# Moving the rounding of the samples between VectorE's two passes in a deformable-convolution block on one Trainium2 core

## The chip, the cores and the metric

The kernel runs on one NeuronCore of one Trainium2 chip. The metric is the device time of one execution in microseconds. Before the change it is 2600.68 us, the median of three runs (2598.38 to 2600.81).

## The reference

For x of shape (4, 128, 80, 80) in float32:

```python
out_normal = _conv(x, w_normal)
offset = jnp.concatenate([_conv(x, w_offx), _conv(x, w_offy)], axis=1)
out_x = _deform_conv(x, offset, w_dx)
out_y = _deform_conv(x, offset, w_dy)
out = _conv(jnp.concatenate([out_normal, out_x, out_y], axis=1), w_fusion)
out = jax.nn.relu(_bn(out, ...))
out = _bn(_conv(out, w_conv2), ...)
return jax.nn.relu(out + x)
```

`_conv` is a 3x3 convolution with padding 1. `_deform_conv` reads, for each pixel and each of nine taps, four neighbouring pixels at a position that the offsets shift, blends them bilinearly and multiplies the blend with that tap's 128x128 weights. Both deformable convolutions use the same offsets, so they share their samples.

## The kernel before

The work goes in strips of 8 rows (640 pixels), 10 strips to an image, 40 in all, and four more steps empty a pipeline: in step i the offsets of strip i+1, the samples and deformable products of strip i, the fusion convolution of strip i-2 and the last convolution of strip i-4 are worked on. Every engine runs a list of its own, written out by hand, and the engines meet at semaphores alone. `run_steps` runs the steps, and inside one, each engine's `step` runs nine **tap steps**, k = 0 to 8. Tap n = 9i + k is counted through all strips.

Values are kept as a rounded high part (fp32r) and a low part (value minus high), and every product is three matmuls (`three`, L388, L391, L394). What happens to tap m of the samples, in five tiles of 128 pixels:

1. GpSimd gathers five tiles of cells from HBM (`gather`, L350, into 15 slots; a slot is free when the mix has read it).
2. The vertical mix, here **mix**: in strips 0 to 9 ScalarE multiplies the upper half (`upper`) and VectorE adds the lower (L756); from strip 10 on the table holds slopes and VectorE does it alone, with five instructions of L756 on 128x256.
3. The horizontal blend: ScalarE multiplies the left half into `samp` (`left`, five products on 128x128), and VectorE adds the right half (L762, five instructions), here **blend**.
4. TensorE turns the five tiles into PSUM (`turn_samples`, L431, tile `turned`), here **turn**.
5. ScalarE rounds `turned` to `samp_hi` (`samples_high`), and VectorE subtracts (`samples_low`, L708) to `samp_lo`, here **low**.
6. TensorE multiplies (`deform_tap`, tile `acc`).

In tap step k, with n = 9i + k, TensorE turns tap n+1, does a slice of the other convolutions (`SLICES`) and multiplies tap n. Its turn waits for two things, the blends of tap n+1 and the low part of tap n, since there is one `turned`:

```python
at_least(eng, samp_done, TILES * n + TILES)
at_least(eng, samp_lo_done, n)
```

In the same tap step ScalarE makes the left products of tap n+2 and the high part of tap n+1, and then what else the step holds (the upper products of tap n+3 in the first image, evacuations of PSUM, the high parts of sums and differences). VectorE mixes and blends tap n+2, takes the low part of tap n+1, and then does the rest of its step: in tap step 3 (2 in the first four steps) `indices` for the next strip, 14 small instructions from L725 to L742, which wait for ScalarE's copy of the offsets (`turned_evac`, tile `off_s`); in tap steps 4 to 7 the sums, differences and their low parts (L832, L708) and the bank evacuations (L929 to L955); in 0 and 1 the residual (L970). The slopes (L832 on `slope`) are made in tap steps 2 and 6 of the first 27 steps. TensorE's second batch of fusion products in tap step 3 reuses the PSUM bank from which `off_s` is copied, so it waits for that copy too.

Of the kernel before, what the change touches and what calls it, by code (L numbers as in the profile page):

```python
# [15 lines left out]
TAPS = 9  # L16
# [122 lines left out]
def at_least(eng, sem, value):  # L139

    if isinstance(value, int) and value <= 0:
        return
    eng.wait_ge(sem, value)


def deform_block(nc, x, xflat, xpair, weights, bn, const, out):
    ctx = ExitStack()
    with ctx:
# [100 lines left out]
        def strip_const(c, n):  # L249
            return cst[:, per_strip + 4 * c + n:per_strip + 4 * c + n + 1]  # L250
# [280 lines left out]
        def _(eng):  # L531
# [45 lines left out]
            def samples_high(n, tp):  # L577
                at_least(eng, samp_turned, n + 1)
                at_least(eng, tap_done, n - 1)
                copy(samp_hi[:, tp], turned[:, 0:PIX]).then_inc(samp_hi_done, 1)  # L580
# [41 lines left out]
            def step(i, par, fl):  # L622
                for k in range(TAPS):
                    n = i * TAPS + k
                    tp = (par + k) % 2
                    if fl.strip and k < TAPS - 2:
                        left(n + 2, k + 2, par, tp)
                    elif fl.strip and fl.nxt:
                        left(n + 2, k + 2 - TAPS, 1 - par, tp)
                    if fl.strip and (k < TAPS - 1 or fl.nxt):  # L630
                        samples_high(n + 1, 1 - tp)
                    if k in fl.weights:
                        weights_high(fl.weights[k])

                    if fl.strip and k < TAPS - 3:
                        upper(n + 3, i, k + 3, par, 1 - tp)
                    elif fl.strip and fl.nxt:
                        upper(n + 3, i + 1, k + 3 - TAPS, 1 - par, 1 - tp)
                    if k == fl.turn and fl.nxt:
                        turned_evac(i + 1)  # L640
                    if k == 1 and fl.last_row:
                        at_least(eng, last_done, i - 1)
                        copy(d_hi[:, :, Z_ROWS - 1, 1:1 + W], d_raw[:, :, Z_ROWS - 1, 1:1 + W])\
                            .then_inc(last_hi, 1)
                    for job, q in fl.done[k]:
                        if job == "O" and fl.nxt:
                            off_evac(i + 1, q)
                        if job == "F" and q == 0 and fl.fuse:
                            s = i - 2
                            at_least(eng, f_done, T * s + 1)  # L650
                            at_least(eng, mid_lo_done, s)
                            eng.activation(mid_odd, work[0][:, 0:HALF].rearrange("p (r w) -> p r w", w=W), ACT.Identity,
                                           bias=scale1[:, 1:2], scale=scale1[:, 0:1]).then_inc(f_one, 1)
                        if job == "F" and q == 1 and fl.rows:
                            sums_high(i - 1)
                        if job == "F" and q == T - 1:
                            s = i - 2
                            if fl.mtop:
                                at_least(eng, mid_lo_done, s)
                                at_least(eng, c_done, 2 * (s - 2) + 2)  # L660
                                copy(mid[:, par, :, 0, 1:1 + W], mid[:, 1 - par, :, ROWS, 1:1 + W].bitcast(F32),
                                     scale=strip_const(s, 2)).then_inc(mtop_done, 1)
                            if fl.fuse:
                                at_least(eng, f_three, s + 1)
                                at_least(eng, f_four, s + 1)
                                at_least(eng, c_done, 2 * (s - 2) + 2)
                                eng.activation(mid[:, par, 0, 1:1 + ROWS, 1:1 + W], mid_f[:], ACT.Relu)\
                                    .then_inc(mid_hi_done, 1)
                            if fl.rows:
                                zs_high(i - 1)  # L670
                            if fl.mbot:
                                at_least(eng, mid_lo_done, s + 1 if fl.fuse else s)
                                at_least(eng, c_done, 2 * (s - 3) + 2)
                                copy(mid[:, 1 - par, :, SLOT_ROWS - 1, 1:1 + W], mid[:, par, :, 1, 1:1 + W].bitcast(F32),
                                     scale=strip_const(s - 1, 3)).then_inc(mbot_done, 1)
                        if job == "N" and fl.strip:
                            rows = slice(q * HR, q * HR + HR)
                            at_least(eng, sums_done, 6 * i)
                            at_least(eng, zs_done, 7 * i)
                            at_least(eng, keep_done, i)  # L680
                            at_least(eng, n_done, 2 * i + q + 1)
                            copy(raw[:, 0, rows, :], work[q][:, 0:HALF].rearrange("p (r w) -> p r w", w=W))\
                                .then_inc(n_out, 1)
                            if q == 1 and fl.load:
                                x_high(i + 2, par)
                        if job == "C" and fl.second:
                            s = i - 4
                            at_least(eng, c_out, 2 * s + q + 1)
                            part = resid[:, q * HALF:(q + 1) * HALF]
                            eng.activation(part, part, ACT.Relu, bias=scale1[:, 3:4]).then_inc(out_ready, 1)  # L690
                if fl.strip:
                    at_least(eng, tap_done, TAPS * i + TAPS)
                    for d in range(2):
                        for half in range(2):
                            rows = slice(half * HR, half * HR + HR)
                            copy(raw[:, 1 + d, rows, :],
                                 acc[2 * d + half][:, 0:HALF].rearrange("p (r w) -> p r w", w=W)).then_inc(acc_out, 1)

            run_steps(eng, step)


# [3 lines left out]
        def _(eng):  # L705
# [36 lines left out]
                eng.tensor_scalar(index[:, par], above[:, 0], strip_const(s, 1), None, ALU.add).then_inc(idx_ready, 1)  # L742
                eng.wait_ge(idx_ready, s + 1)

            def sample(n, k, par, tp):

                for j in range(TILES):
                    g, turns = (k * TILES + j) % GSLOTS, (k * TILES + j) // GSLOTS + 1
                    both = mixed[:, tp, j].rearrange("p (x c) -> p x c", x=2)
                    base = both  # L750
                    if n < STRIPS * TAPS:
                        at_least(eng, upper_done, TILES * n + j + 1)
                    else:
                        at_least(eng, cells_in[g], (PER // GSLOTS * 16) * (n // TAPS) + 16 * turns)
                        base = corner[:, g, :, 0, :]
                    eng.scalar_tensor_tensor(  # L756
                        out=both, in0=corner[:, g, :, 1, :], scalar=wgt[:, par, 1, 0, j, k:k + 1], in1=base,
                        op0=ALU.mult, op1=ALU.add,
                    ).then_inc(mixed_done, 1)
                for j in range(TILES):  # L760
                    at_least(eng, left_done, TILES * n + j + 1)
                    eng.scalar_tensor_tensor(  # L762
                        out=samp[:, tp, j], in0=mixed[:, tp, j, C:2 * C],
                        scalar=wgt[:, par, 1, 1, j, k:k + 1], in1=samp[:, tp, j], op0=ALU.mult, op1=ALU.add,
                    ).then_inc(samp_done, 1)

            def samples_low(n, tp):
                at_least(eng, samp_hi_done, n + 1)
                low(samp_lo[:, tp], turned[:, 0:PIX], samp_hi[:, tp]).then_inc(samp_lo_done, 1)
# [29 lines left out]
            eng.wait_ge(cst_in, 16)  # L799
            indices(0, 0)  # L800
            weights_low(W_DEF)
            sample(0, 0, 0, 0)
            x_low(1, 1)
            sample(1, 1, 0, 1)
            samples_low(0, 0)

            eng.wait_ge(bn_in, 16)
# [92 lines left out]
            def step(i, par, fl):  # L900
                for k in range(TAPS):
                    n = i * TAPS + k
                    tp = (par + k) % 2
# [1 line left out]
                        last_row(i - 2)  # L905

                    if fl.strip and k < TAPS - 2:
                        sample(n + 2, k + 2, par, tp)
                    elif fl.strip and fl.nxt:
                        sample(n + 2, k + 2 - TAPS, 1 - par, tp)  # L910
                    if fl.strip and (k < TAPS - 1 or fl.nxt):
                        samples_low(n + 1, 1 - tp)
                    if k in fl.transform:
                        weights_form()
# [117 lines left out]
```

## Time and profile before

| what | value |
|---|---|
| median of three runs | 2600.68 us |
| the profiled execution, its time | 2602.97 us |
| its span | 2601.2 us |
| mean granted TensorE clock (share of full) | 0.961 |
| busy: TensorE matmul / weight load | 91% / 89% |
| busy: VectorE / ScalarE / GpSimd | 87% / 60% / 74% |
| mean DMA rate | 217 GB/s |

Busy shares are averages over the span. Rows of the timeline give the start, the busy time and, in brackets, the idle time of the engine before the instruction with what ended it. Consecutive instructions of one engine overlap in their records, so the step from one start to the next is shorter than the busy time.

### The profile page before, as it was taken

The numbers are of one execution on the slowest core, as the hardware profiler recorded it, in microseconds if no ns is written. First come the engines' busy times: TensorE is split into PE (matmuls) and PEld (weight loads), VectorE is DVE, ScalarE is ACT, GpSimd is POOL, SyncE is SP. The second block draws the span as 40 slices with busy tenths as digits, with TensorE's granted clock in tenths as the row PEclk, the third lists the DMA queues.
The fourth block names the chain that finished last, engine by engine and source line by source line (L and its number), as shares of the span: only waits on it lengthen the run. The fifth ranks groups of instructions, "written<-read, shape, count | busy, mean of one in ns | idle before, by whom it ended". The sixth has DMA issues, their size and how long they took to land.

```text
span 2601.2 us, 47091 instructions
## 1 busy us (share of the span) xinstructions
PE 2355.7 (91%) x15680; PEld 2319.4 (89%) x15680; DVE 2265.0 (87%) x5999; ACT 1561.9 (60%) x3577; POOL 1917.4 (74%) x1807
## 2 busy tenths in 40 slices
PE   3668999999999999999999999999999998999997
PEld 3668889898999999998999999999999998999997
DVE  5788988888999999999999989999999998999962
ACT  5777888778555555555555555555555555555531
POOL 7777777777777777777777777777777777777730
PEclk7789999999999999999999999999999999999998
DMA  7767777777777777777777777777777667776630
GB/s 232 220 208 219 235 228 231 232 231 229 227 237 233 231 234 237 233 236 232 236 237 237 234 237 239 238 222 210 209 209 217 206 208 212 210 210 210 202 111 26
DMA packets 179139, 564.90 MB, mean 217 GB/s; under 512 B 32720, under 2 KB 34128, under 8 KB 178768
## 3 DMA queue, kind: packets, MB, share of 16 engines
q0 software_dynamic: 144000, 471.97, 60.3%
q1 hardware_dynamic: 34896, 89.91, 10.1%
q8 instruction: 125, 2.05, 0.3%
q14 instruction: 118, 0.97, 0.1%
HBM read 527.41 MB, written 34.34 MB: 216 GB/s over the span
## 4 chain that ended last, share of the span: by engine, by line
DVE 46%; PE 23%; ACT 15%; issue 8%; DMA 5%; POOL 2%; ACTq 0%; DVEq 0%; SPq 0%; POOLq 0%
DVE mixed L756 11%; DVE d_lo L708 7%; DVE d_lo_f L832 7%; DVE samp L762 6%; ACT samp L535 6%; PE work L388 5%; PE work L394 5%; PE work L391 5%; DMA cells<-slope_table,index 4%; DVE samp_lo L708 4%; ACT samp_hi L534 3%; ACT mixed L535 3%; PE turned L431 2%; POOL cells L350 2%; PE acc L388 2%
## 5 line engine op out<-in xcount | busy, mean ns | idle before, releaser
L350 POOL DMA_INDIRECT cells<-slope_table,index x1350 | 1434.0, 1062 | 414.1 <-issue 223.3
L535 ACT ACTIVATE samp<-mixed,wgt 128x128 f32<-128x128 f32 x1800 | 644.6, 397 | 492.6 <-DVE mixed L756 490.8
L350 POOL DMA_INDIRECT cells<-in_xpair,index x450 | 473.7, 1053 | 166.6 <-issue 83.4
L756 DVE SCALAR_TENSOR_TENSOR mixed<-cells,wgt 128x256 f32<-128x256 f32 x1350 | 560.9, 477 | 39.2 <-DMA cells<-slope_table,index 37.9
L762 DVE SCALAR_TENSOR_TENSOR samp<-mixed,wgt,samp 128x128 f32<-128x128 f32 x1800 | 513.8, 345 | 39.1 <-ACT samp L535 38.8
L388 PE MATMUL work<-d_hi,w_hi 128*128 128x320 f32 x1440 | 467.9, 325 | 22.0 <-ACT off_s L534 19.7
L391 PE MATMUL work<-d_lo,w_hi 128*128 128x320 f32 x1440 | 452.8, 314 | 0.0
L394 PE MATMUL work<-d_hi,w_lo 128*128 128x320 f32 x1440 | 452.3, 314 | 0.0
L388 PE MATMUL acc<-samp_hi,w_hi 128*128 128x320 f32 x1440 | 450.2, 313 | 0.0
L391 PE MATMUL acc<-samp_lo,w_hi 128*128 128x320 f32 x1440 | 448.4, 311 | 0.0
L394 PE MATMUL acc<-samp_hi,w_lo 128*128 128x320 f32 x1440 | 446.9, 310 | 0.0
L431 PE MATMUL turned<-cst,samp 128*128 128x128 f32 x1800 | 267.2, 281 | 194.6 <-DVE samp_lo L708 176.8
L431 PEld LDWEIGHTS turned<-cst,samp 128*128 128x128 f32 x1800 | 214.9, 143 | 223.1 <-issue 151.8
L708 DVE TENSOR_TENSOR samp_lo<-turned,samp_hi 128x640 fp32r<-128x640 f32 x360 | 294.3, 818 | 47.6 <-ACT samp_hi L534 47.6
L388 PEld LDWEIGHTS work<-d_hi,w_hi 128*128 128x128 f32 x1440 | 272.4, 189 | 27.8 <-ACT off_s L534 25.2
L534 ACT ACTIVATE d_hi<-d_lo_f 128x1920 fp32r<-128x1920 f32 (+2 forms) x120 | 153.2, 1277 | 237.7 <-DVE d_lo_f L832 230.9
L388 PEld LDWEIGHTS acc<-samp_hi,w_hi 128*128 128x128 f32 x1440 | 275.9, 192 | 0.0
L391 PEld LDWEIGHTS acc<-samp_lo,w_hi 128*128 128x128 f32 x1440 | 274.9, 191 | 0.0
L394 PEld LDWEIGHTS acc<-samp_hi,w_lo 128*128 128x128 f32 x1440 | 274.8, 191 | 0.0
L391 PEld LDWEIGHTS work<-d_lo,w_hi 128*128 128x128 f32 x1440 | 273.3, 190 | 0.0
L394 PEld LDWEIGHTS work<-d_hi,w_lo 128*128 128x128 f32 x1440 | 272.7, 189 | 0.0
L534 ACT ACTIVATE samp_hi<-turned 128x640 fp32r<-128x640 f32 x360 | 247.8, 688 | 13.4 <-PE turned L431 11.9
(86 smaller groups left out, 4279.3 us busy)
## 6 DMA issues: line engine op xcount, KB each, us to landing
cells<-slope_table,index POOLq DMA_INDIRECT x1350, 3.9
slope<-in_xpair SPq DMA_DIRECT2D x54, 384.0 KB, 5.3
slope_table<-slope SPq DMA_DIRECT2D x54, 384.0 KB, 4.1
x_raw<-in_xflat SPq DMA_DIRECT2D x40, 410.0 KB, 4.1
resid<-in_x SPq DMA_DIRECT2D x40, 320.0 KB, 5.3
out<-resid SPq DMA_DIRECT2D x40, 320.0 KB, 3.9
cells<-in_xpair,index POOLq DMA_INDIRECT x450, 3.8
w_lo_f<-in_weights SPq DMA_DIRECT2D x4, 576.0 KB, 7.9
```

The lines of the kernel that those rows point to most:

```text
L350: eng.indirect_dma_start(out=cells[:, g, :], out_offset=None, in_=cell_rows, in_offset=bass.IndirectOffsetOnAxis(ap=index[:, par, j, k:k + ...
L388: ins = eng.matmul(dst, w_hi[:, w], hi, start=start, stop=False, skip_group_check=True)
L391: ins = eng.matmul(dst, w_hi[:, w], lo, start=False, stop=False, skip_group_check=True)
L394: return eng.matmul(dst, w_lo[:, w], hi, start=False, stop=stop, skip_group_check=True)
L431: ins = eng.transpose(turned[:, j * 128:(j + 1) * 128], samp[:, tp, j, :], ident)
L534: return eng.activation(dst, src, ACT.Copy)
L535: return eng.activation(dst, src, ACT.Copy, scale=scale)
L708: return eng.tensor_tensor(dst, src, hi.bitcast(F32), ALU.subtract)
L756: eng.scalar_tensor_tensor(out=both, in0=corner[:, g, :, 1, :], scalar=wgt[:, par, 1, 0, j, k:k + 1], in1=base, op0=ALU.mult, op1=ALU.add, ...
L762: eng.scalar_tensor_tensor(out=samp[:, tp, j], in0=mixed[:, tp, j, C:2 * C], scalar=wgt[:, par, 1, 1, j, k:k + 1], in1=samp[:, tp, j], op0 ...
L832: return eng.scalar_tensor_tensor(out=dst, in0=a, scalar=1.0, in1=b, op0=ALU.mult, op1=op)
```

## The change

No instruction is added or taken away, and TensorE's, GpSimd's and SyncE's lists stay as they are. `sample` is cut into `mix` (the loop with L756) and `blend` (the loop with L762 before, L765 after). VectorE takes the low part of tap n+1 between mix and blend of tap n+2, and ScalarE rounds tap n+1 before it makes the left products of tap n+2. The three taps ahead of the first step keep their order.

```diff
                     tp = (par + k) % 2
+                    if fl.strip and (k < TAPS - 1 or fl.nxt):
+                        samples_high(n + 1, 1 - tp)
                     if fl.strip and k < TAPS - 2:
                         left(n + 2, k + 2, par, tp)
                     elif fl.strip and fl.nxt:
                         left(n + 2, k + 2 - TAPS, 1 - par, tp)
-                    if fl.strip and (k < TAPS - 1 or fl.nxt):
-                        samples_high(n + 1, 1 - tp)
...
                     if fl.strip and k < TAPS - 2:
-                        sample(n + 2, k + 2, par, tp)
+                        mix(n + 2, k + 2, par, tp)
+                        samples_low(n + 1, 1 - tp)
+                        blend(n + 2, k + 2, par, tp)
                     elif fl.strip and fl.nxt:
-                        sample(n + 2, k + 2 - TAPS, 1 - par, tp)
-                    if fl.strip and (k < TAPS - 1 or fl.nxt):
+                        mix(n + 2, k + 2 - TAPS, 1 - par, tp)
+                        samples_low(n + 1, 1 - tp)
+                        blend(n + 2, k + 2 - TAPS, 1 - par, tp)
+                    elif fl.strip and k < TAPS - 1:
                         samples_low(n + 1, 1 - tp)
```

VectorE in tap steps 2 and 3 of a strip from the eleventh on, before (`resid` closes tap step 1, L725 opens the indices; mixed is the mix, samp the blend):

```order
L970 SCALAR_TENSOR_TENSOR resid<-work1,scale1,resid 128x320
L756 SCALAR_TENSOR_TENSOR mixed<-cells,wgt 128x256 x5
L762 SCALAR_TENSOR_TENSOR samp<-mixed,wgt,samp 128x128 x5
L708 TENSOR_TENSOR samp_lo<-turned,samp_hi 128x640
L708 TENSOR_TENSOR d_lo<-d_lo_f,d_hi 128x3x80
L832 SCALAR_TENSOR_TENSOR slope<-slope 128x3x128
L756 SCALAR_TENSOR_TENSOR mixed<-cells,wgt 128x256 x5
L762 SCALAR_TENSOR_TENSOR samp<-mixed,wgt,samp 128x128 x5
L708 TENSOR_TENSOR samp_lo<-turned,samp_hi 128x640
L725 TENSOR_TENSOR off_s<-off_s 128x5x18
```

and the same place after the change:

```order
L979 SCALAR_TENSOR_TENSOR resid<-work1,scale1,resid 128x320
L756 SCALAR_TENSOR_TENSOR mixed<-cells,wgt 128x256 x5
L708 TENSOR_TENSOR samp_lo<-turned,samp_hi 128x640
L765 SCALAR_TENSOR_TENSOR samp<-mixed,wgt,samp 128x128 x5
L708 TENSOR_TENSOR d_lo<-d_lo_f,d_hi 128x3x80
L837 SCALAR_TENSOR_TENSOR slope<-slope 128x3x128
L756 SCALAR_TENSOR_TENSOR mixed<-cells,wgt 128x256 x5
L708 TENSOR_TENSOR samp_lo<-turned,samp_hi 128x640
L765 SCALAR_TENSOR_TENSOR samp<-mixed,wgt,samp 128x128 x5
L725 TENSOR_TENSOR off_s<-off_s 128x5x18
```

The five blends have moved behind the low part, in every tap step; what follows the group of three is where it was.

ScalarE at the same place, before (L535 is the left products, `samp_hi` the high part, `off_s` the copy of the offsets):

```order
L534 ACTIVATE off_c<-work0 32x320 x3
L535 ACTIVATE samp<-mixed,wgt 128x128 x5
L534 ACTIVATE samp_hi<-turned 128x640
L534 ACTIVATE off_c<-work1 32x320 x3
L535 ACTIVATE samp<-mixed,wgt 128x128 x5
L534 ACTIVATE samp_hi<-turned 128x640
L534 ACTIVATE off_s<-work1 128x270
L652 ACTIVATE mid_f<-work0,scale1 128x4x80
```

and after:

```order
L534 ACTIVATE off_c<-work0 32x320 x3
L534 ACTIVATE samp_hi<-turned 128x640
L535 ACTIVATE samp<-mixed,wgt 128x128 x5
L534 ACTIVATE off_c<-work1 32x320 x3
L534 ACTIVATE samp_hi<-turned 128x640
L535 ACTIVATE samp<-mixed,wgt 128x128 x5
L534 ACTIVATE off_s<-work1 128x270
L652 ACTIVATE mid_f<-work0,scale1 128x4x80
```

The five left products now stand behind the rounding, and so between it and the copy of the offsets.

## Rows read from the trace of the kernel before

**Rows 1.** The page, part 1: busy time, share of the span, instructions of each engine.

```profile
PE 2355.7 (91%) x15680; PEld 2319.4 (89%) x15680; DVE 2265.0 (87%) x5999; ACT 1561.9 (60%) x3577; POOL 1917.4 (74%) x1807
```

**Rows 2.** The page, part 4: the chain that ended last, shares by engine.

```profile
DVE 46%; PE 23%; ACT 15%; issue 8%; DMA 5%; POOL 2%; ACTq 0%; DVEq 0%; SPq 0%; POOLq 0%
```

**Rows 3.** Waits over the whole span: waiter, releaser, us in total, times, longest.

```profile
PE turned L431 <- DVE samp_lo L708: 176.8, 105, 11.9
...
DVE samp_lo L708 <- ACT samp_hi L534: 47.6, 139, 2.1
DVE samp L762 <- ACT samp L535: 38.8, 79, 2.4
```

**Rows 4.** Timeline of TensorE: first turn and one wait of tap steps, strips apart.

```profile
702.97 0.71 PE L431 MATMUL turned<-cst,samp 128*128 128x128 f32 x5
...
1500.66 0.71 PE L431 MATMUL turned<-cst,samp 128*128 128x128 f32 x5
...
1503.95 0.41 PE L388 MATMUL work<-d_hi,w_hi 128*128 128x320 f32 x1 [0.78 <-ACT off_s L534]
...
1563.14 0.71 PE L431 MATMUL turned<-cst,samp 128*128 128x128 f32 x5
...
1569.96 0.71 PE L431 MATMUL turned<-cst,samp 128*128 128x128 f32 x5
...
1597.24 0.74 PE L431 MATMUL turned<-cst,samp 128*128 128x128 f32 x5 [2.54 <-DVE samp_lo L708]
...
1624.16 0.71 PE L431 MATMUL turned<-cst,samp 128*128 128x128 f32 x5
...
2422.44 0.71 PE L431 MATMUL turned<-cst,samp 128*128 128x128 f32 x5
```

**Rows 5.** Timeline of VectorE, two strips of the third image.

```profile
1501.92 0.52 DVE L756 SCALAR_TENSOR_TENSOR mixed<-cells,wgt 128x256 f32<-128x256 f32 x1 [2.32 <-DMA cells<-slope_table,index]
...
1504.41 0.24 DVE L725 TENSOR_TENSOR off_s<-off_s 128x90 f32<-128x90 f32 x1
...
1562.41 1.39 DVE L762 SCALAR_TENSOR_TENSOR samp<-mixed,wgt,samp 128x128 f32<-128x128 f32 x5
1564.62 0.82 DVE L708 TENSOR_TENSOR samp_lo<-turned,samp_hi 128x640 fp32r<-128x640 f32 x1 [0.82 <-ACT samp_hi L534]
1565.37 0.24 DVE L725 TENSOR_TENSOR off_s<-off_s 128x90 f32<-128x90 f32 x1
...
1570.72 1.40 DVE L762 SCALAR_TENSOR_TENSOR samp<-mixed,wgt,samp 128x128 f32<-128x128 f32 x5
1572.04 0.81 DVE L708 TENSOR_TENSOR samp_lo<-turned,samp_hi 128x640 fp32r<-128x640 f32 x1
...
1578.59 1.52 DVE L762 SCALAR_TENSOR_TENSOR samp<-mixed,wgt,samp 128x128 f32<-128x128 f32 x5 [0.19 <-ACT samp L535]
1580.35 0.82 DVE L708 TENSOR_TENSOR samp_lo<-turned,samp_hi 128x640 fp32r<-128x640 f32 x1 [0.23 <-ACT samp_hi L534]
...
1588.24 0.55 DVE L832 SCALAR_TENSOR_TENSOR slope<-slope 128x384 f32<-128x384 f32 x1
...
1596.27 0.82 DVE L708 TENSOR_TENSOR samp_lo<-turned,samp_hi 128x640 fp32r<-128x640 f32 x1 [0.23 <-ACT samp_hi L534]
```

**Rows 6.** Timeline of ScalarE, tap step 3 of the same second strip.

```profile
1560.99 1.93 ACT L535 ACTIVATE samp<-mixed,wgt 128x128 f32<-128x128 f32 x5 [0.82 <-DVE mixed L756]
1563.89 0.70 ACT L534 ACTIVATE samp_hi<-turned 128x640 fp32r<-128x640 f32 x1 [0.96 <-PE turned L431]
1564.49 0.39 ACT L534 ACTIVATE off_s<-work 128x270 f32<-128x270 f32 x1
```

**Rows 7.** The page, part 5: GpSimd's gathers from the slope table.

```profile
L350 POOL DMA_INDIRECT cells<-slope_table,index x1350 | 1434.0, 1062 | 414.1 <-issue 223.3
```

**Rows 8.** Timelines of TensorE and VectorE, tap step 3 in the first image.

```profile
513.46 0.71 PE L431 MATMUL turned<-cst,samp 128*128 128x128 f32 x5
...
517.50 0.26 DVE L725 TENSOR_TENSOR off_s<-off_s 128x90 f32<-128x90 f32 x1 [1.44 <-ACT off_s L534]
```

More of the change, by code:

```diff
@@ L743, in indices, with mix @@
                 eng.wait_ge(idx_ready, s + 1)
-            def sample(n, k, par, tp):
+            def mix(n, k, par, tp):
                 for j in range(TILES):
@@ L759, in sample, with blend @@
                     ).then_inc(mixed_done, 1)
+            def blend(n, k, par, tp):
                 for j in range(TILES):
@@ L801, in _ @@
             weights_low(W_DEF)
-            sample(0, 0, 0, 0)
+            mix(0, 0, 0, 0)
+            blend(0, 0, 0, 0)
             x_low(1, 1)
-            sample(1, 1, 0, 1)
+            mix(1, 1, 0, 1)
+            blend(1, 1, 0, 1)
             samples_low(0, 0)
```

## The prediction

> **What bounds the kernel now.** I read the busy shares first: TensorE 91%, VectorE 87%, GpSimd 74% [rows 1], none of them full. The chain that ended last runs through VectorE for 46% and TensorE for 23% [rows 2], so the two take turns. The waits say where: TensorE's turn waits 176.8 us for the low part, which is the last thing that VectorE does for it; VectorE waits 47.6 us for the rounding and 38.8 us for the left products [rows 3]. These 86.4 us are what the change is after.
>
> The timelines show the two handovers of a strip. In tap step 3 TensorE is the late one: the turn starts at 1563.14, ScalarE has been idle 0.96 us for it and rounds at 1563.89, VectorE has been idle 0.82 us and takes the low part at 1564.62, 1.48 us after the turn [rows 4 to 6]. From there VectorE is late and hardly rests (indices, sums, differences), until TensorE waits 2.54 us in tap step 8, at 1597.24 [rows 4]. Then TensorE paces again until the next turn of tap step 3, at 1624.16: one strip is 61.02 us. Call v the time from that turn to the first instruction of the indices. Here v is 1565.37 - 1563.14 = 2.23. In the strip before it VectorE's last mix of the tap waited 2.32 us for its cells, and v is 1504.41 - 1500.66 = 3.75, with a strip of 62.48 [rows 4, 5]. In both the strip is 58.7 or 58.8 plus v. So **whatever is put between the turn of tap step 3 and the indices is paid in full**, once a strip, although both engines have idle time elsewhere.
>
> There is a second pace. GpSimd's 1350 gathers of images 2 to 4 take 1434.0 us and 414.1 us of gaps, of which 223.3 are ended by nothing that the profile shows [rows 7]; 45 gathers are (1434.0 + 414.1) / 1350 x 45 = 61.6 us. Over the 28 strips from 702.97 to 2422.44 the mean strip is 61.41 us [rows 4]. So GpSimd is at its own pace there, and the late cells are its way of holding VectorE back. The Trainium skill (Perfetto Trace Analysis, Identifying the Most-Contended Engine) would judge GpSimd by its occupancy, which is 74% and would leave it a quarter free; by that no strip needs over 61.0, and the loss below would count from 61.0, 0.4 us a strip more. The trace disagrees: the gaps between gathers return with every one of them.
>
> **The change, part by part.** Instruction counts are the same, so only waits count.
>
> *VectorE, tap step 3.* Before, the five blends (1570.72 to 1572.04, 1.32 us [rows 5]) ran from 1562.41, while TensorE and ScalarE were getting the rounding ready: free work in front of a wait. Now VectorE has only the mix ahead of the low part. It stands from 1562.41 to the same 1564.62, since the low part still needs the turn, 1.48 us earlier; then come 0.75 us of low part and only then 1.32 us of blends, ahead of the indices. v goes from 2.23 to 3.55: **+1.32**. In strips where v was already 3.75 because cells were late, the mix ends after the rounding, and the order costs nothing; that is why the mean before, and not 61.02, is what I subtract.
>
> *ScalarE, tap step 3.* Its left products were done before the turn (1560.99 [rows 6]); now they stand behind the rounding, about 1.5 us for five when nothing holds them back, and the copy of the offsets, at 1564.49 before, ends near 1566.4, 3.3 us after the turn. The indices come 3.55 after it, so they are not held. TensorE's second fusion batch is: in the strip where the copy ended 3.3 us after the turn, it stood 0.78 us (1503.95 [rows 4]). I take 0.9. That moves the next turn from 1569.96 to 1570.9; its low part can start 1.48 later, at 1572.35, where VectorE ends its mix at 1570.72 + 1.32 = 1572.04. That is **+0.3**; the ends are 0 and 0.9. The rest of TensorE's 0.9 us falls into its 2.54 us wait of tap step 8.
>
> *Tap steps 5 and 7.* Here ScalarE comes late from the high parts of the sums and differences. VectorE waited 0.19 and 0.23 in step 5, where the blends also ran 1.52 instead of 1.40, and 0.23 in step 7 [rows 5]. Now the rounding goes first behind those parts, 0.6 us, and the low part waits that long in step 5 and some 0.15 in step 7, the blends after it no more. I work out -0.16 and -0.19, together **-0.35**; the ends are 0 and -0.77 (all four).
>
> *Other tap steps.* In 0 to 2 the low part also waits more for its turn (blends no longer cover), but VectorE has over 1 us to spare there, in front of TensorE; in 8 the mix, about 2 us, covers turn and rounding, 1.48. Zero.
>
> *GpSimd.* Same list; a strip that is longer than 61.6 gives it rest. Zero, and the late cells should go.
>
> The sum for a strip of images 2 to 4: 61.02 + 1.32 + 0.3 - 0.35 = 62.3; less 0.2, since 11 of the 28 strips have no slope instructions (0.55 us [rows 5]): 62.1. Against 61.41 that is +0.7, and 28 strips give **+20 us**.
>
> *First image.* The indices already wait 1.44 us for the copy of the offsets, 4.04 us after the turn [rows 8], because ScalarE does the rounding and the upper products first. Now the left products stand in that row too: +1.5, less 0.3 because the rounding no longer waits for them, and the rest as above: +1.3 a strip for the five steady strips, **+7 us**. The first four strips, where VectorE is late all round and an offset copy (tap step 2) comes behind longer rows on ScalarE, I take at 0, between -1.3 and +1.3 each.
>
> Total +27: the profiled execution would go from 2602.97 to 2630. The median of the runs lies 2.3 us lower than that execution, so I say **2628 us** (+1.0%).
>
> **Rivals.**
> 1. *GpSimd's pace covers it.* If the low part in step 3 comes only 0.5 us late, or the waits in steps 5 and 7 vanish wholly (-0.77) and step 4 costs nothing, the strip is 61.6, GpSimd's pace, and VectorE's loss takes the place of late cells. For it: many of the 28 strips already have a v over 2.8. Against: v = 3.55 is above nearly all of them. Images 2 to 4 cost 28 x 0.2 = 5, the first 0 to 3: 2601 to 2609.
> 2. *Faster: the low part frees TensorE sooner.* The turn's 176.8 us are booked to the low part. The Trainium skill (Perfetto Trace Analysis, Optimization Strategy) says to find the gaps of the contended engine, see which semaphore ends them, and make that dependency start sooner; this edit does that to the letter. Here it would take the 0.77 us of waits off VectorE's late stretch with nothing put back, if the turn of step 3 came early enough (0.8 us sooner than 1563.14) for the low part to follow the mix. GpSimd holds images 2 to 4 at 61.6, so it pays in 14 strips, the first ten and the four at the start of image 2: 14 x 0.77 = 11, 2590. Against it: the turn waits for blend and low part both, and their sum ends no earlier; and the turn of step 3 waits for nobody, TensorE is simply not there yet.
> 3. *The waits only change names.* The low part's wait before the blends is what the blends' wait was before: within 5 us of 2601. Against: the period follows v.
> 4. *Worse: the short cover bites in every tap.* If the low part lags in tap steps 0 to 2 and 8 also, and TensorE's 0.9 is not absorbed, a strip takes 1 us more than above: 2628 + 38 = 2666.
>
> **How the numbers follow.** Forecast 0.64, rival 1 0.15, rival 2 0.08, rival 3 0.08, rival 4 0.05. The forecast's own spread comes from 0 to 0.9 and 0 to -0.77 in 28 strips, -12 to +17, and the first image, +-5: 2610 to 2645. The range takes in rival 1 as well and leaves out rivals 2 and 4: 2601 to 2643. A difference of 0.2% (5.2 us) is what a measurement of this kernel can tell. Faster is rival 2: 0.08. Within 0.2% lie rival 3 and over half of rival 1: 0.17. Slower is the rest: 0.75.
>
> **What the profile after would show.** Right: strips of images 2 to 4 of about 62 us with v near 3.5 in nearly all, VectorE's low part waiting for the rounding over 100 us in total instead of 47.6, its waits for left products under 20, late cells nearly gone, GpSimd with true waits (for the mix or TensorE), TensorE waiting for the copy of the offsets in nearly every strip, and its turn released by the blend instead of the low part. Wrong: strips at 61.4 or less (rivals 1 to 3), or a v that grows while the strip doesn't, which would mean that VectorE's stretch from step 3 to 8 isn't what ends last.

## The result and the profile after

| what | before | after |
|---|---|---|
| median | 2600.74 us (4 runs, 2598.38 to 2601.13) | 2635.55 us (4 runs, 2632.79 to 2642.39) |
| the profiled execution, its time | 2602.97 us | 2632.79 us |
| its span | 2601.2 us | 2631.0 us |
| granted TensorE clock | 0.961 | 0.963 |

The ratio is 1.0141, with a 95% interval of 1.0123 to 1.0160. The forecast was 2628 us, in a range of 2601 to 2643, with a chance of 0.75 for slower.

The page of the changed kernel, parts 1 and 4:

```profile
PE 2360.8 (90%) x15680; PEld 2313.8 (88%) x15680; DVE 2245.5 (85%) x5999; ACT 1511.2 (57%) x3577; POOL 1913.1 (73%) x1807
...
DVE 43%; PE 41%; ACT 9%; issue 5%; POOL 1%; DMA 1%; ACTq 0%; DVEq 0%; SPq 0%
```

The busy times are within about 5 us of those of [rows 1] for TensorE and GpSimd, and lower by 20 and 51 us for VectorE and ScalarE, so it is waits that were added; TensorE's share of the chain has gone from 23% [rows 2] to 41%, and DMA (the late cells) from 5% to 1%. Now the waits over the whole span, as in [rows 3]:

```profile
ACT samp_hi L534 <- PE turned L431: 489.4, 211, 7.5
...
DVE samp_lo L708 <- ACT samp_hi L534: 198.4, 188, 3.4
...
PE turned L431 <- DVE samp L765: 188.7, 101, 17.4
...
PE work L388 <- ACT off_s L534: 43.4, 37, 3.0
...
PE turned L431 <- DVE samp_lo L708: 7.4, 1, 7.4
...
DVE samp L765 <- ACT samp L535: 0.4, 1, 0.4
```

VectorE's 38.8 us for the left products are gone, and its 47.6 us for the rounding have become 198.4. TensorE's turn is now released by the blend. For blend and low part together it waits 188.7 + 7.4 = 196.1 us, where it was 176.8 + 17.3 = 194.1 before (the 17.3 are one wait for the blend): the low part was never more than the last of two things that the turn needed. All that the prediction wrote down as signs of being right has come.

One strip, first TensorE's timeline (start, busy, idle before and its releaser), turns of tap steps 3, 4, 8 and again 3:

```profile
1582.76 0.71 PE L431 MATMUL turned<-cst,samp 128*128 128x128 f32 x5
...
1585.99 0.42 PE L388 MATMUL work<-d_hi,w_hi 128*128 128x320 f32 x1 [0.73 <-ACT off_s L534]
...
1590.56 0.71 PE L431 MATMUL turned<-cst,samp 128*128 128x128 f32 x5
...
1618.17 0.77 PE L431 MATMUL turned<-cst,samp 128*128 128x128 f32 x5 [2.51 <-DVE samp L765]
...
1645.11 0.71 PE L431 MATMUL turned<-cst,samp 128*128 128x128 f32 x5
```

ScalarE in tap step 3 of the same strip:

```profile
1583.50 0.70 ACT L534 ACTIVATE samp_hi<-turned 128x640 fp32r<-128x640 f32 x1 [3.02 <-PE turned L431]
1584.10 1.56 ACT L535 ACTIVATE samp<-mixed,wgt 128x128 f32<-128x128 f32 x5
1585.57 0.38 ACT L534 ACTIVATE off_s<-work 128x270 f32<-128x270 f32 x1
```

VectorE, the low parts of tap steps 3, 4 and 5, and the start of the indices:

```profile
1584.24 0.82 DVE L708 TENSOR_TENSOR samp_lo<-turned,samp_hi 128x640 fp32r<-128x640 f32 x1 [1.47 <-ACT samp_hi L534]
1584.98 1.39 DVE L765 SCALAR_TENSOR_TENSOR samp<-mixed,wgt,samp 128x128 f32<-128x128 f32 x5
1586.29 0.24 DVE L725 TENSOR_TENSOR off_s<-off_s 128x90 f32<-128x90 f32 x1
...
1592.04 0.82 DVE L708 TENSOR_TENSOR samp_lo<-turned,samp_hi 128x640 fp32r<-128x640 f32 x1 [0.47 <-ACT samp_hi L534]
...
1600.22 0.82 DVE L708 TENSOR_TENSOR samp_lo<-turned,samp_hi 128x640 fp32r<-128x640 f32 x1 [0.49 <-ACT samp_hi L534]
```

The low part still starts 1.48 us after the turn, the blends now follow, and v, from turn to indices, is 1586.29 - 1582.76 = 3.53 us (2.23 and 3.75 in [rows 4, 5]). In the 29 strips from the eleventh, v lies between 3.53 and 3.54 in every one. This strip takes 1645.11 - 1582.76 = 62.35 us, which is v plus 58.8, the same 58.8 as before (two effects cancel in it, see below). The copy of the offsets starts 2.8 us after the turn, TensorE stands 0.73 us for it, and the next turn comes 7.80 us after this one (1590.56) where it was 6.82 (1569.96 less 1563.14, [rows 4] and the prediction). The mean over the same 28 strips as in [rows 4]:

```profile
709.58 0.71 PE L431 MATMUL turned<-cst,samp 128*128 128x128 f32 x5
...
2451.19 0.71 PE L431 MATMUL turned<-cst,samp 128*128 128x128 f32 x5
```

(2451.19 - 709.58) / 28 = 62.20 us, against 61.41: +22 us over the 28. The turn at which they begin comes 6.6 us later than before. Together that is all but one of the 29.8 us between the two spans. GpSimd's row, to be read against [rows 7]:

```profile
L350 POOL DMA_INDIRECT cells<-slope_table,index x1350 | 1429.5, 1059 | 437.8 <-issue 232.2
```

Its gaps have grown by 24 us, because it has real waits now, for the mix or for TensorE (`gather` waits also for a semaphore `pace`, which keeps it within five taps of TensorE's products): 32 gathers stand more than 0.4 us, where before the change 1346 of 1350 followed the one before them by 0.30 to 0.32 us. Waits of VectorE for late slope cells don't occur any more.

### The profile page after: what moved, and what is told of

Its sections match the earlier page's. It is cut to its first block, busy times and chain, and to the rows that moved or that the text cites. A ratio compares the mean times of both kernels' runs of the same rounds, so it can differ in the third digit from the quotient of the medians.

```text
span 2631.0 us, 47091 instructions
## 1 busy us (share of the span) xinstructions
PE 2360.8 (90%) x15680; PEld 2313.8 (88%) x15680; DVE 2245.5 (85%) x5999; ACT 1511.2 (57%) x3577; POOL 1913.1 (73%) x1807
## 4 chain that ended last, share of the span: by engine, by line
DVE 43%; PE 41%; ACT 9%; issue 5%; POOL 1%; DMA 1%; ACTq 0%; DVEq 0%; SPq 0%
DVE samp L765 9%; PE work L388 8%; DVE mixed L756 8%; DVE d_lo_f L837 7%; PE work L394 7%; PE work L391 7%; DVE d_lo L708 7%; DVE samp_lo L708 6%; PE turned L431 4%; PE work L373 4%; PE acc L388 3%; PE acc L391 3%; PE acc L394 3%; ACT samp_hi L534 3%; ACT samp L535 2%
## 5 line engine op out<-in xcount | busy, mean ns | idle before, releaser
L350 POOL DMA_INDIRECT cells<-slope_table,index x1350 | 1429.5, 1059 | 437.8 <-issue 232.2
L535 ACT ACTIVATE samp<-mixed,wgt 128x128 f32<-128x128 f32 x1800 | 597.6, 396 | 102.8 <-DVE mixed L756 102.8
L756 DVE SCALAR_TENSOR_TENSOR mixed<-cells,wgt 128x256 f32<-128x256 f32 x1350 | 556.8, 477 | 1.2 <-DVE index L742 0.2
L388 PE MATMUL work<-d_hi,w_hi 128*128 128x320 f32 x1440 | 471.3, 327 | 44.0 <-ACT off_s L534 43.4
L765 DVE SCALAR_TENSOR_TENSOR samp<-mixed,wgt,samp 128x128 f32<-128x128 f32 x1800 | 501.5, 343 | 0.4 <-ACT samp L535 0.4
L708 DVE TENSOR_TENSOR samp_lo<-turned,samp_hi 128x640 fp32r<-128x640 f32 x360 | 295.4, 820 | 202.3 <-ACT samp_hi L534 198.4
L431 PE MATMUL turned<-cst,samp 128*128 128x128 f32 x1800 | 271.1, 283 | 199.3 <-DVE samp L765 188.7
```

What stands on the lines that cost most here:

```text
L350: eng.indirect_dma_start(out=cells[:, g, :], out_offset=None, in_=cell_rows, in_offset=bass.IndirectOffsetOnAxis(ap=index[:, par, j, k:k + ...
L388: ins = eng.matmul(dst, w_hi[:, w], hi, start=start, stop=False, skip_group_check=True)
L431: ins = eng.transpose(turned[:, j * 128:(j + 1) * 128], samp[:, tp, j, :], ident)
L535: return eng.activation(dst, src, ACT.Copy, scale=scale)
L708: return eng.tensor_tensor(dst, src, hi.bitcast(F32), ALU.subtract)
L756: eng.scalar_tensor_tensor(out=both, in0=corner[:, g, :, 1, :], scalar=wgt[:, par, 1, 0, j, k:k + 1], in1=base, op0=ALU.mult, op1=ALU.add, ...
```

## The experiments

"Mean strip" below is always the time from the turn of tap step 3 in the eleventh strip to that in the thirty-ninth, divided by 28, read as above. Each set of runs had its own runs of the kernel before, with medians from 2598.0 to 2601.2 us.

### The old order in the tap step of the indices

The new order stays in the other eight tap steps. ScalarE's half of the edit is alike; the cuts of code here and below are shortened to the calls that move.

```diff
+                    if k == fl.turn:
+                        mix(...)
+                        blend(...)
+                        samples_low(n + 1, 1 - tp)
+                    else:
                         mix(...)
                         samples_low(n + 1, 1 - tp)
                         blend(...)
```

> The change, but the tap step of the indices (3, or 2 in the first four steps) keeps the order of before on both engines; the eight others have the new order. Theory (what stands between the turn of that step and the indices is paid once a strip): the indices start 2.2 us after the turn again where cells aren't late, both engines together allow a strip of 61.0 - 0.35 = 60.7 us, and GpSimd's pace holds images 2 to 4 at 61.4 as before; the late cells return. 2594 to 2603 us. Rival (every tap pays for its shorter cover, or the loss is in the other steps): strips stay near 62.2 and the time near 2632 us.

Measured: 2616.1 us (4 runs), ratio 1.0070 (1.0053 to 1.0086), mean strip 61.61 us. Between the two: half of the 14.7 us between the profiled spans of this kernel and of the one before the change lies in the first image (7.0 us, up to the turn of the eleventh strip). A strip without late cells, TensorE and VectorE in order of time:

```profile
771.35 0.71 PE L431 MATMUL turned<-cst,samp 128*128 128x128 f32 x5
...
778.16 0.71 PE L431 MATMUL turned<-cst,samp 128*128 128x128 f32 x5
...
832.68 0.71 PE L431 MATMUL turned<-cst,samp 128*128 128x128 f32 x5
```

```profile
773.57 0.24 DVE L733 TENSOR_TENSOR off_s<-off_s 128x90 f32<-128x90 f32 x1
...
779.65 0.82 DVE L716 TENSOR_TENSOR samp_lo<-turned,samp_hi 128x640 fp32r<-128x640 f32 x1 [0.73 <-ACT samp_hi L534]
```

v is back at 2.22, so the theory holds for it; but the strip takes 61.33 us, 59.1 plus v, not the 58.5 that I had worked out. The second fence shows where: in tap step 4 VectorE's low part stands 0.73 us, until 1.49 us after the turn at 778.16. With the indices early again, VectorE has done only its mix when it reaches that low part, and TensorE is the late one once more. **There are two handovers, one step apart**, and before the change the blends covered both. The steady strips of the first image took 65.0 us; there TensorE stands 1.87 us for the copy of the offsets, and the low part of the next tap step stands 2.17 us.

### Two old steps, and fewer gathers

To see the engines' own pace, three kernels leave out five of the 45 gathers of a strip from the eleventh strip on, those of the ninth tap, which is then blended from old cells: the kernel before, the changed kernel, and the changed kernel with the old order in the tap step of the indices and the one behind it.

```diff
+def skipped(c, q):
+    return c >= STRIPS and q // TILES == TAPS - 1
...
                 for q in range(PER):
+                    if skipped(c, q):
+                        continue
```

> The kernel before, without the five gathers of the ninth tap in strips 10 to 39 (40 of 45 remain; that tap is blended from old cells). Theory (GpSimd's pace of 61.6 us a strip holds images 2 to 4): the late cells vanish, strips are 61.0 us where slopes are made and 60.5 after, 2583 to 2591 us. Rival (GpSimd isn't a bound, the late cells are DMA latency): 2600 us, late cells stay.

Measured: 2581.45 us (4 runs), ratio 0.9930 (0.9903 to 0.9958), mean strip 60.79. The page's row of GpSimd and the first and last turn:

```profile
L364 POOL DMA_INDIRECT cells<-slope_table,index x1200 | 1270.9, 1059 | 549.5 <-issue 191.7
```

```profile
701.38 0.71 PE L445 MATMUL turned<-cst,samp 128*128 128x128 f32 x5
...
2403.63 0.71 PE L445 MATMUL turned<-cst,samp 128*128 128x128 f32 x5
```

No wait for late slope cells is left, and the strips are 60.8 to 61.1 us with slopes and about 60.5 without. So GpSimd's pace did hold images 2 to 4 of the kernel before, for 28 x (61.41 - 60.79) = 17 us, though the page shows it at 74%. Its gaps say the same: before, 4 of 1350 gathers from the slope table stood over 0.4 us; here 121 of 1200 do, 184 us in all. From issue to landing the cells take 3.8 us in the median against 3.9, so it isn't that they landed faster.

> The changed kernel with the same five gathers left out. Theory: its strips of 62.36 us aren't set by GpSimd, so nothing moves: 2630 to 2636 us, strips 62.3 to 62.4. Rival (GpSimd still holds it, or fewer gathers speed up other things): strips shorter by 0.3 us or more.

Measured: 2637.69 us in one run, 1.7 us over the range, mean strip 62.24 (62.20 with all gathers). The changed kernel isn't held by GpSimd.

> The new order, but the order of before in the tap step of the indices and the one after it; and without the five gathers of the ninth tap in strips 10 to 39 (that tap is blended from old cells), so that GpSimd's pace doesn't hide the rest. Theory (there is a second handover one step later: behind the indices VectorE reaches its low part before TensorE's next turn allows it, unless the blends stand in front; it cost 0.73 us in the run with one old step): both covers are back, only the gain of tap steps 5 and 7 is left, and strips are 60.94 - 0.3 = 60.65 us where slopes are made, 60.2 after; the steady strips of the first image go from 65.0 to 63.0 us. Rival (the 0.7 us come from the steps that keep the new order): strips stay near 61.35 us, the first image at 65.

Measured: 2572.23 us in one run.

```profile
1246.69 0.71 PE L445 MATMUL turned<-cst,samp 128*128 128x128 f32 x5
...
1307.32 0.71 PE L445 MATMUL turned<-cst,samp 128*128 128x128 f32 x5
```

The strip is 60.63 us, 0.3 less than the kernel before without those gathers (mean strip 60.51 against 60.79), as the theory has it. The first image's steady strips are 62.7 to 63.7, on average 63.3: that is where they were before the change, and the gain expected there (63.0) didn't come. With the two covers back, the new order loses nothing and gains 0.3 us a strip in images 2 to 4. This run has the new order in tap steps 0 to 2 and 5 to 8; that the gain is that of 5 and 7 is shown further down.

### Each half alone

The first kernel keeps VectorE's new order and gives ScalarE its old one, as below; the second keeps ScalarE's new order and lets VectorE run mix, blend and low part as before.

```diff
-                    samples_high(n + 1, 1 - tp)
                     left(n + 2, ...)
+                    samples_high(n + 1, 1 - tp)
```

> Only VectorE's half of the change; ScalarE keeps left products before the rounding. Theory: the time from turn to indices is still 3.5 us, TensorE no longer stands for the copy of the offsets, but in tap steps 4 to 8, where VectorE is late, the low part now stands about 1.1 us each for left products and rounding that can only follow the mix: strips near 67 us, 2760 to 2840 us in all. Rival (ScalarE's half makes the loss, through the late copy of the offsets): at most 2610 us.

Measured: 2883.03 us in one run, mean strip 68.75. More than expected: VectorE waits 493.6 us for the rounding, in 359 low parts, so in every tap step and not only in 4 to 8, with 1.4 us each. v is 4.2 to 4.4 in strips with slopes, but the strips are 64.8 us plus v and not 58.8: most of this loss lies outside the stretch from turn to indices.

```profile
DVE samp_lo L708 <- ACT samp_hi L534: 493.6, 359, 3.0
```

> Only ScalarE's half; VectorE keeps mix, blend, low. Theory: in the tap step of the indices the left products stand behind the rounding and so behind the turn, the blends behind them, so the indices start 3.9 us after the turn, a little later than with both halves, and steps 5 and 7 gain nothing: strips of 63.2 us, about 2660 us. Rival (the loss is VectorE's order alone): 2601 to 2610 us.

Measured: 2680.19 us in one run, mean strip 63.51, v 3.94. The blends wait 238.8 us for left products that stand behind the rounding. Here the strips are 59.8 plus v, since TensorE waits for the copy of the offsets as well (43.4 us, as in the changed kernel). The two halves belong together: each alone is worse than both. They lose in different ways. With ScalarE's half alone the blends end behind the turn, as in the changed kernel and 0.4 us later; with VectorE's half alone every low part stands for left products and rounding.

### The copy of the offsets ahead of the left products

```diff
                     samples_high(n + 1, 1 - tp)
+                    if k == fl.turn and fl.nxt:
+                        turned_evac(i + 1)
                     left(n + 2, ...)
...
-                    if k == fl.turn and fl.nxt:
-                        turned_evac(i + 1)
```

> The change, and ScalarE copies the offsets right behind the rounding, ahead of the left products. Theory: the time from turn to indices stays 3.53 us in images 2 to 4; only TensorE's wait of 0.73 us goes, and with it about 0.35 us of the low part's wait in tap step 4: strips of 62.0 instead of 62.36 us. In the first image, where the indices waited for the copy, it goes from 5.21 to about 3.55 us and strips shrink by about 2.2 us. In all 2603 to 2612 us. Rival (the 0.73 us of TensorE are wholly on the path): 61.6 us strips, below 2600; or not on it at all: 62.36 us strips and only the first image faster, 2618 us.

Measured: 2601.91 us (10 runs), ratio 1.0012 (1.0003 to 1.0022), mean strip 61.94. v stays 3.53 where cells aren't late, TensorE doesn't wait for the copy, and the strips before late cells set in are 61.8 us. A strip in order of time, three turns of TensorE:

```profile
871.57 0.71 PE L431 MATMUL turned<-cst,samp 128*128 128x128 f32 x5
...
878.38 0.71 PE L431 MATMUL turned<-cst,samp 128*128 128x128 f32 x5
...
933.41 0.71 PE L431 MATMUL turned<-cst,samp 128*128 128x128 f32 x5
```

The next turn is back at 6.81 us, and the low part of tap step 4 no longer waits. The late copy thus cost 0.5 us a strip, where I had counted 0.35. Later strips are at 61.4 to 62.8, with late cells back: GpSimd is full again. None of its 1350 gathers from the slope table stands longer than 0.32 us, and they take 1074 ns each instead of 1062, so its pace is (1449.7 + 411.4) / 1350 x 45 = 62.0 us a strip, and the mean strip is at it. In the first image v went from 5.21 to 3.53 and the steady strips from 65.3 (mean of four) to 61.8, more than the 2.2 expected. The time is nearly that of the kernel before, but the loss isn't undone: images 2 to 4 still lose 28 x (61.94 - 61.41) = 15 us, v is as long as before this edit, and the first image wins 16.8 us (its end, the turn of the eleventh strip, comes at 686.22 instead of 702.97). The next run shows that this gain has nothing to do with the change.

### The same copy in the kernel before, and the new order where it gains

The kernel before, with the copy moved ahead of the upper products:

```diff
+                    if k == fl.turn and fl.nxt:
+                        turned_evac(i + 1)
...
                     if fl.strip and k < TAPS - 3:
                         upper(n + 3, ...)
...
-                    if k == fl.turn and fl.nxt:
-                        turned_evac(i + 1)
```

> The kernel before, and ScalarE copies the offsets ahead of the upper products. In images 2 to 4 there are no upper products, so nothing moves. In the first image the indices start about 2.6 us after the turn instead of 4.04, and each of its steady strips loses 1.4 us: 2588 to 2593 us. Rival (ScalarE is the bound there, the upper products are only late next): 2598 to 2601 us.

Measured: 2585.74 us (7 runs), ratio 0.9945 (0.9929 to 0.9962). The steady strips of the first image take 61.8 instead of 63.3 us, with v 2.5 instead of 4.05; the mean strip of the rest is 61.40, as it was. The eleventh strip's turn comes at 685.91, so the first image's gain is that of the copy alone. This kernel beats both, and against it the change with the same copy costs about 16 us (2601.91 us).

> The kernel before with the offsets copied ahead of the upper products, once more, on the same chip as the kernel that also takes the new order in tap steps 5 to 8: 2583 to 2588 us, as in its first run.

Measured: 2586.33 us (5 runs), ratio 0.9947 (0.9933 to 0.9960).

Then the new order on top, in tap steps 5 to 8:

> The kernel before with the offsets copied ahead of the upper products, and the new order in tap steps 5 to 8 alone, where ScalarE came late. All gathers are there. Engines alone would allow 0.3 us a strip less; theory: GpSimd's pace (61.4 to 61.6 us a strip) takes that back in images 2 to 4, and the first image's strips go from 61.8 to 61.5: 0 to 3 us less than the same kernel without the new order in 5 to 8, 2581 to 2586 us. Rival (GpSimd's pace doesn't bind): 11 us less, 2575 us.

Measured: 2631.16 us (4 runs), ratio 1.0116 (1.0101 to 1.0132), mean strip 63.05. Wrong, and neither theory's number: 45 us more. VectorE waits 130.5 us for late slope cells. The page's rows of GpSimd, first of the kernel with the copy moved, then of this one:

```profile
L350 POOL DMA_INDIRECT cells<-slope_table,index x1350 | 1432.8, 1061 | 411.3 <-issue 219.7
L350 POOL DMA_INDIRECT cells<-in_xpair,index x450 | 480.2, 1067 | 146.6 <-issue 84.1
```

```profile
L350 POOL DMA_INDIRECT cells<-slope_table,index x1350 | 1481.4, 1097 | 411.4 <-issue 214.5
L350 POOL DMA_INDIRECT cells<-in_xpair,index x450 | 482.8, 1073 | 145.2 <-issue 73.4
```

The gathers take 51.2 us more in all, their gaps 1.3 us less, and the span is 2633.0 against 2582.3 us, 50.7 more. GpSimd has no slack there (none of the 1350 stands longer than 0.32 us), so its longer instructions are the whole loss. Two long ones come in each strip, 59 over 2 us in all; the kernel with the copy moved has 26, one of 2.6 us in most strips:

```profile
1549.68 2.21 POOL L350 DMA_INDIRECT cells<-slope_table,index  x1 [0.30 <-issue]
1552.19 2.99 POOL L350 DMA_INDIRECT cells<-slope_table,index  x1 [0.30 <-DVE mixed L764]
```

The commonest take 0.95 us. To see whether tap step 8 makes them, the new order was kept in 5 and 7 alone:

> As the kernel with the offsets copied first and the new order in tap steps 5 to 8, but in 5 and 7 alone. In that run GpSimd's gathers from the slope table took 1097 ns each instead of 1061, 49 us in all, with two gathers of 2 to 3 us in each strip around the passage from tap step 8 to 0. Theory A (they come from the new order in step 8, where VectorE's and ScalarE's work now lies differently beside the gathers): with the old order in 8 the gathers are back at 1062 ns and the time at 2581 to 2586 us. Theory B (they come whenever VectorE and TensorE are earlier in steps 5 and 7): 1090 ns and 2620 to 2635 us.

Measured: 2602.66 us (10 runs), ratio 1.0017 (1.0006 to 1.0029), gathers 1073 ns. Between the theories, so neither is shown: the pair of long gathers is gone (21 over 2 us in all, one in a strip at most), but the mean isn't back at 1062. The account of GpSimd holds here too: its gathers (1447.9 and 486.7 us) take 21.6 us more than with the copy moved alone, and the span of 2604.2 us is 21.9 longer. In four kernels no gather from the slope table stands longer than 0.32 us: this one, the one above it, the change with the copy moved, and the kernel before with the copy moved. Their pace, busy time and gaps of 45 gathers, is 61.97, 63.09, 62.04 and 61.47 us, and their mean strips are 61.88, 63.05, 61.94 and 61.40.

The strips that no late cell touches show what tap steps 5 and 7 are worth by themselves. One of them:

```profile
753.82 0.71 PE L431 MATMUL turned<-cst,samp 128*128 128x128 f32 x5
...
814.61 0.71 PE L431 MATMUL turned<-cst,samp 128*128 128x128 f32 x5
```

It takes 60.79 us; those with slopes and a v of 2.22 take 60.7 to 60.9, and 61.0 to 61.1 with the copy moved alone. So 0.3 us a strip is the gain of these two, which GpSimd takes back elsewhere.

## Why the prediction was right, and where its steps were off

**The mechanism and the sign.** Forecast: the blends leave their place in front of a wait and go behind it, v grows by 1.32 us and is paid in full, once a strip. Measured: v +1.30 against the strip of 2.23, at 3.53 in every strip of images 2 to 4. The run with one old step brought v back, the one with two old steps brought the strip back. That the lost cover makes the loss is shown.

**The price.** That a strip is v plus 58.8 after the change too is luck: in the changed kernel v isn't what ends last. VectorE still stands 0.47 us in tap step 4 for the rounding, so what holds it there is TensorE's next turn, which comes 0.98 us later. With the copy early and v left (the run with the copy moved), the strip lost 0.5 us and was 58.3 plus v. With the copy early and v brought back, 1.31 us less (the run with one old step), it lost only another 0.5 and was 59.1 plus v, since the low part of tap step 4 then stands 0.73 us. So the law read from two strips of the kernel before, where late cells move v, doesn't give the price in the kernels after it. The sum (1.32 + 0.3 - 0.35 = 1.27) came out at 1.33 because it had the second term as well.

**Tap step 4.** I put it at +0.3, as a by-product of TensorE's wait for the copy. It was +0.47 in VectorE's wait (1592.04): this term was too small by a third. And it is more than a by-product: it is a second handover, hidden behind the first. With only the first repaired it costs 0.73 us, without any wait for the copy. I had said that tap steps 0 to 2 and 8 have cover and had not asked what happens in 4 once VectorE is early again.

**Tap steps 5 and 7.** -0.35 forecast. VectorE before the change, in the strip of [rows 5], the mix of step 5 and what follows the group, then the same for step 7:

```profile
1576.34 2.06 DVE L756 SCALAR_TENSOR_TENSOR mixed<-cells,wgt 128x256 f32<-128x256 f32 x5
...
1581.09 0.54 DVE L938 SCALAR_TENSOR_TENSOR mid_f<-work,scale,mid_f 128x320 f32<-128x320 f32 x1
...
1592.64 2.06 DVE L756 SCALAR_TENSOR_TENSOR mixed<-cells,wgt 128x256 f32<-128x256 f32 x5
...
1597.01 2.50 DVE L708 TENSOR_TENSOR d_lo<-d_lo_f,d_hi 128x320 fp32r<-128x320 f32 x6
```

and after it:

```profile
1597.67 2.06 DVE L756 SCALAR_TENSOR_TENSOR mixed<-cells,wgt 128x256 f32<-128x256 f32 x5
...
1602.28 0.54 DVE L947 SCALAR_TENSOR_TENSOR mid_f<-work,scale,mid_f 128x320 f32<-128x320 f32 x1
...
1613.82 2.06 DVE L756 SCALAR_TENSOR_TENSOR mixed<-cells,wgt 128x256 f32<-128x256 f32 x5
...
1618.04 2.50 DVE L708 TENSOR_TENSOR d_lo<-d_lo_f,d_hi 128x320 fp32r<-128x320 f32 x6
```

4.75 us have become 4.61, and 4.37 have become 4.22: -0.14 and -0.15 for the -0.16 and -0.19 worked out. The strips of the last run above give 0.3 for the two. The size was right.

**Images 2 to 4.** 62.1 and +20 us forecast, 62.20 and +22 measured. GpSimd's 61.6 was 0.2 over the mean strip that it was said to set; four gathers that really waited make half of that. The subtraction of the mean 61.41, and not of what the engines alone allow, was needed: the runs with fewer gathers show 60.79 for the engines of the kernel before and no shorter strip for the kernel after. By the Trainium skill's occupancy rule (Perfetto Trace Analysis, Identifying the Most-Contended Engine) GpSimd, at 74%, would not have been looked at, and the forecast would have been about 11 us higher, an estimate from the 0.4 us a strip of the prediction. The rows disagree with the rule here: GpSimd held the kernel, with a gap of 0.30 us in front of nearly every gather and nothing else.

**The first image.** +7 forecast, +6.6 measured, but from terms that cancel. From the turn of the sixth strip's tap step 3 to that of the tenth, strips went from 63.3 to 65.3 us, +2.1 each where I had +1.3; v grew by 1.16 there, and TensorE stands 2.73 us for the copy instead of 1.57. With the strip behind them the five came to +11.2 us where I had +6.5. The strips ahead of them, which I took at 0, came out 4.6 us shorter. Kernels with the same order in those strips differ there by 1 to 2 us, so scatter doesn't make all of it, and what does I haven't explained. That the total fits is luck.

**The baseline.** I set the median 2.3 us under the profiled execution. After the change the profiled execution was the fastest of four (2632.79), so the median stands 2.8 over it. Of the 7.5 us by which the forecast was low, 2.8 are the sum's (2630 against 2632.79 for the profiled execution) and the rest is this.

**Rivals.** That GpSimd's pace would cover the loss was wrong for the reason given: v is above nearly all that late cells made of it (5 of the 28 strips before had a v of 3.56 or more), and the strip is above GpSimd's pace. The faster case rested on freeing the turn sooner; its wait changed its releaser and stayed as long, 196.1 us against 194.1 for both releasers together. The Trainium skill's advice (Perfetto Trace Analysis, Optimization Strategy) is to find the semaphore or semaphores that a gap waits on and make them come sooner. This edit did so for one of two; the rows show that the gap stayed with the other.

## What to carry to other kernels

When two engines hand over to each other in turns, work that one of them does in front of its wait is free, and the same work behind the wait is paid for, in full unless a later handover ends last anyway (here 1.3 us of v brought back alone gave 0.5): before moving a step across a wait, look which engine is late at that place, and not which one idles more over the span. Measure the period from a fixed event to the wait's successor in two neighbouring rounds; if the period follows it one for one, that stretch is the place to leave alone. Then look one handover further: it can be covered by the same work. An engine whose instructions all follow each other with the same short gap (0.30 us here) is full, whatever its share says, and a gain elsewhere is worth nothing until it has slack.

## What was not expected of the hardware

A gather's time on GpSimd depends on what the other engines do beside it. In the kernels with all gathers these instructions are the same; their mean from the slope table was 1062 ns before and 1059 after the change, 1061 (twice), 1067, 1073 and 1074 in others and 1097 in one, where it cost 50 us. In the two kernels with half the change it was 1043 and 1035, and in those with 40 gathers a strip 1059, 1075 and 1110. The long gathers of 2 to 3 us lie near the passage from tap step 8 to 0 and 1, where x and slopes are loaded and VectorE reads x. In the kernel with 1097 ns they stay in the last strips, which move no slopes, so the slope transfers don't make them.

The rows say which engine it is. In the kernel before, VectorE ran nothing beside 39 of the 1350 gathers, and beside 41 more only instructions that read a tile of PSUM (`turned`, `work` or `acc`, which TensorE writes): all 80 took 0.94 to 0.96 us. It is so in all thirteen kernels, 25 to 57 gathers of the first kind and 29 to 108 of the second, none over 0.96. Every longer gather, and so each one over 2 us (26 before, 59 in the kernel with 1097 ns), ran at least in part beside VectorE instructions that read only SBUF, where all other tiles lie, such as mix, blend and the low part of x; many others beside such instructions took 0.95 us all the same. The order in which VectorE works thus moves GpSimd's pace, by 1.6 us a strip between 1061 and 1097 ns. That is read from the traces; no run was made for it, and what sets the length of those that are held isn't known.
